# Moving the resolvents ahead in the prologue of a fused convolution, state-space and mixture-of-experts kernel

## The chip, the cores and the metric

The kernel runs on one core of a Trainium2 chip. The core's engines run their own instruction streams and meet only at semaphores: TensorE (PE in the profile), VectorE (DVE), ScalarE (ACT), GpSimd (POOL) and SyncE (SP), which issues most of the DMA transfers. The metric is the device time of one launch in microseconds; lower is better. All inputs are float32, and nearly every matrix product is made from three matmuls on high and low parts.

## The reference, cut to what matters

```python
x = x + attn(cond(x, style), Lambda, p, q, Vc, Ct, Bp, D, log_step)   # x: 64 x 64 x 1024
x = x + ffn(cond2(x, style), W_base, b_base, W_router, A, B)          # top 2 of 8 experts, LoRA rank 16

def cond(x, style):                 # 4 modulated convolutions: same, up (x2, blur), same, blur + down
    for i, typ in enumerate(TYPES):
        s = style @ mw[i].T + mb[i]
        weight = SCALE * w[i] * s[:, None, :, None]
        weight = weight * rsqrt(sum(weight ** 2) + EPS)
        x = conv(x, weight, typ) + b[i]

def s4_kernel(Lambda, p, q, B, Ct, step, L):        # inside attn, once for all rows
    Omega = exp(-2j * pi * arange(L) / L)
    g, c = 2 / step * ((1 - Omega) / (1 + Omega)), 2 / (1 + Omega)
    denom = g[:, None] - Lambda[None, :]            # 1024 roots x 64 states, complex
    cauchy = lambda v: (v[None, :] / denom).sum(-1) # four of them: k00, k01, k10, k11
    return ifft(c * (k00 - k01 / (1 + k11) * k10)).real
```

Attention is a long causal convolution of each row with this kernel K, which the program does as products with a Toeplitz matrix of K.

## The kernel before, in words

The 64 samples of the first block (`cond` and the state-space convolution) are taken in 32 tiles of two, then again 32 tiles for the second block (`cond2` and the experts). A tile g passes through a software pipeline whose steps have one function per engine with the same name: `scaled1` and `step1` and `composed1` and `step2` and `composed_out` build that tile's composed weights (taps), DMA moves them into `vm_f`, `composed2` splits them into `vm_h` and `vm_l`; `inputs` scales and splits the input into `xs_h` and `xs_l`; `layer0` makes the first convolution; `pair` and `third` the composed rest; `turn` transposes; `s4` applies the Toeplitz matrix. The main loop `body(i)` of every engine runs i from 1 to 65. What comes before it is written out by hand, one list of calls per engine named `first_turns` (GpSimd has its list ahead of and in `body(-1)`), and the order of each list is the order on that engine. That prologue also does what is needed only once:

- The style tables `tabs` (scales, and shifts by `shifts`), and a chain for the bias constants: three small TensorE products `constant(0, 0)`, `(0, 1)`, `(0, 2)` with the weights summed over their taps (`wsum`, made by GpSimd in `tap_sums` and `tap_sums_end`), each followed by `through(0, l)` on VectorE, which makes the right side of the next product.
- The edge columns, in four TensorE steps `edge_pe0` to `edge_pe3`, each followed by VectorE's `edge_ve0` to `edge_ve3`. `edge_ve0` ends in the pads, which `edge_pads_first` splits; its semaphore `apad_ready` is what ScalarE's `layer0(0)` waits for. The folds of the edge matrices `em` are GpSimd's `folded(1)` and `folded(2)`.
- The state-space kernel: `denominators` and `denominators_turned` (VectorE) make the complex denominators, ScalarE squares them, `resolvents` adds the squares and takes the reciprocal, `resolvents_scaled` makes `res`, TensorE's `resolved` sums over the states (eight products of 128x128 with 16 columns), VectorE's `transfer` (some 40 instructions of 8 columns) combines them, then TensorE and VectorE alternate in `transform`, `twiddles`, `twisted`, `transposed`, `second_transform` and `kernel_out`.

GpSimd's order for tile 1 is `inputs(1)` (writes `xs_l`), `column_sums_low(0)` (`as_l`), `pair_sums(0)` (`vm_f`), `pair_sums_low(0)` (`vs_l`). ScalarE's order after its `layer0(0)` is `composed1(1)`, `composed2(0)`, `inputs(1)`, `inputs_high(1)`, `column_sums(0)`, `pads(0)`, `pair_sums(0)`, `pair_evacuated(0, 0)`.

Of the kernel before, what the change touches and what calls it, by code (L numbers as in the profile page):

```python
# [404 lines left out]
def program(nc, d, out, sb, sem, sh):  # L405
# [57 lines left out]
    with ExitStack() as early:  # L463
        def tb(name, shape, dt=F32):
# [71 lines left out]
    mats_hi, mats_lo = sem("mats_hi"), sem("mats_lo")  # L536
    rate_ready, rate_out, den_ready, sq_ready, res_ready = (sem("rate_ready"), sem("rate_out"), sem("den_ready"),
                                                            sem("sq_ready"), sem("res_ready"))
    pe_F, at_ready, pe_dft, z_ready, pe_zT, zT_ready, pe_K, k_ready = (
        sem("pe_F"), sem("at_ready"), sem("pe_dft"), sem("z_ready"), sem("pe_zT"), sem("zT_ready"), sem("pe_K"), sem("k_ready"))  # L540
    zero_set, k_out, toep_in, pe_toep = sem("zero_set"), sem("k_out"), sem("toep_in"), sem("pe_toep")
# [71 lines left out]
    def turn_is(i, *which):  # L613
        return i in which
# [77 lines left out]
    with nc.Block() as block:  # L692
# [126 lines left out]
        def _(pool):  # L819
# [34 lines left out]
            def tap_sums(c):  # L854

                pool.wait_ge(fold_in, 32)
                for l, s in enumerate(summed(c)):
                    for h in range(2):
                        ins = G.tensor_tensor(wsum[:, l, c, h, :], s[:, 0, :], s[:, 1, :], ALU.add)
                ins.then_inc(wsum_step, 1)  # L860
# [77 lines left out]
            def body(i):  # L938
# [34 lines left out]
                if turn_is(i, 9):  # L973
                    r_low(1)
                if turn_is(i, -1):
                    pool.wait_ge(in_lo, 1)
                    tap_sums(0)
                    tap_sums_end(0)
                    folded(1, fold1())
                    folded(2, fold3())  # L980

                    inputs(1)
                    column_sums_low(0)
                    pair_sums(0)
                else:
                    if here(i + 1):
                        pair_sums(i + 1)
                        column_sums_low(i + 1)
                    if here(i + 2):
                        inputs(i + 2)  # L990
# [4 lines left out]
        def _(act):  # L995
# [170 lines left out]
            def first_turns():  # L1166
# [4 lines left out]
                inputs_high(0)  # L1171
                composed1(0)
                edge_lay_first(nc, act, sh)
                terms_of(fold1()[2:])
                act.wait_ge(den_ready, 1)
                A(tmp, den, ACT.Square).then_inc(sq_ready, 1)
                scaled1(1)
                terms_of(fold3())
                layer0(0)
# [87 lines left out]
        def _(ve):  # L1267
# [139 lines left out]

            def resolvents():
                ve.wait_ge(sq_ready, 1)
                link(V.tensor_tensor(tmp[:, 0, :], tmp[:, 0, :], tmp[:, 1, :], ALU.add))  # L1410
                link(V.reciprocal(tmp[:, 1, :], tmp[:, 0, :]))

            def resolvents_scaled():
# [215 lines left out]
            def first_turns():  # L1629
# [15 lines left out]
                edge_scale(nc, ve, sh, 0, xgA[:, 0:EB, :])  # L1645
                denominators()
                composed1(0)
                shifts(0)
                state_vectors()
                denominators_turned()  # L1650
                through(0, 0)
                composed_out(0)
                scaled1(1)
                edge_ve0(nc, ve, sh, 0, ps_p)
                edge_pads_first(nc, ve, sh)
                through(0, 1)
                resolvents()
                through(0, 2)
                state_halves()
                composed1(1)  # L1660
                resolvents_scaled()
                layer0(0)
                composed2(0)
                transfer()
                edge_ve1(nc, ve, sh, 0, ps_p)
                twiddles()
# [102 lines left out]
        def _(pe):  # L1769
# [184 lines left out]
            def first_turns():  # L1954

                step1(0)
                constant(0, 0)
                step2(0)
                edge_pe0(nc, pe, sh, 0, ps_p)
                layer0(0)  # L1960
                constant(0, 1)
                pe.wait_ge(blur, at(0))
                step1(1)
                constant(0, 2)
                pe.wait_ge(folds, 1)
                edge_pe1(nc, pe, sh, 0, ps_p)
                resolved()
                pair(0, 0)
                step2(1)
                pair(0, 1)  # L1970
# [143 lines left out]
```

## Time and profile before

| | |
|---|---|
| time, median of 3 runs | 1338.35 us (1337.68 to 1340.94) |
| the profiled execution's own time | 1339.31 us, span in the trace 1337.5 us |
| PE busy | 1295.4 us, 97% |
| DVE busy | 1044.6 us, 78% |
| ACT and POOL busy | 798.4 and 807.0 us, 60% each |
| granted TensorE clock, mean | 0.994 of full speed |

The span is cut in 40 slices of 33.4 us in the page. In the first three TensorE is busy for 3, 7 and 8 tenths, and from the fourth on for 9 tenths or more. A row of the timeline has the start and the duration in us, then engine, line, operation, written and read tile, their shapes and the count; in brackets the idle time before it and who ended it. Durations of neighbours overlap a little, since an instruction's end is counted when its writes have landed. A row of the windows view gives a stretch, the busy time of each engine, and the granted TensorE clock (1.00 is 2.4 GHz, 0.50 is 1.2 GHz).

### The profile page before, as it was taken

How to read it: one execution, taken by the hardware profiler on the slowest of the kernel's cores; microseconds unless marked ns; L12 is line 12 of the kernel's file. 1: busy time of each engine (PE TensorE's matmuls, PEld its weight loads, DVE VectorE, ACT ScalarE, POOL GpSimd, SP SyncE). 2: the span in 40 equal slices, each digit the busy share in tenths (PEclk: the TensorE clock that was granted, in tenths of full speed). 3: DMA queues.
4: the chain of work that ended last, by engine and by line, in shares of the span. 5: the costliest groups of instructions: out<-in, count | busy, mean ns of one | idle time of the engine just before them, and what ended most of it. 6: DMA issues, size and time to landing. Idle time of an engine off the chain costs nothing.

```text
span 1337.5 us, 22885 instructions
## 1 busy us (share of the span) xinstructions
PE 1295.4 (97%) x8127; PEld 1227.3 (92%) x8127; DVE 1044.6 (78%) x2442; ACT 798.4 (60%) x1625; POOL 807.0 (60%) x611
## 2 busy tenths in 40 slices
PE   3789999999999999999999999999999999999998
PEld 2689899899899999899999999999999999999998
DVE  7868878778877778778788888787878878787873
ACT  4577787778777787775545544555554454555440
POOL 6468887666676677665555545554555555545542
PEclk9889999999999999999999999999999999999999
DMA  4234444444455654452542523425243342524422
GB/s 133 74 107 132 133 133 133 133 132 133 132 146 150 151 152 134 133 154 78 125 110 91 141 77 108 124 77 153 78 127 105 100 131 78 147 85 122 110 86 87
DMA packets 86274, 158.20 MB, mean 118 GB/s; under 512 B 26633, under 2 KB 48402, under 8 KB 86034
## 3 DMA queue, kind: packets, MB, share of 16 engines
q1 hardware_dynamic: 84898, 154.79, 41.8%
q10 hardware_dynamic: 1264, 1.96, 0.5%
q8 instruction: 65, 1.06, 0.4%
q14 instruction: 47, 0.39, 0.1%
HBM read 93.79 MB, written 33.56 MB: 95 GB/s over the span
## 4 chain that ended last, share of the span: by engine, by line
PE 84%; DVE 7%; POOL 4%; ACT 3%; issue 1%; DMA 0%; SPq 0%; DVEq 0%; POOLq 0%; ACTq 0%
PE psum L1775 27%; PE psum L1777 26%; PE psum L1776 26%; PE psum L1889 2%; DVE psum L1549 2%; POOL xs_l L931 1%; ACT xin L1104 1%; DVE a_l L1525 1%; DVE a_f L1530 1%; POOL vs_l L926 0%; POOL vbuf L910 0%; POOL vbuf L906 0%; PE psum L283 0%; POOL as_l L935 0%; ACT xs_h L1109 0%
## 5 line engine op out<-in xcount | busy, mean ns | idle before, releaser
L1775 PE MATMUL psum<-wt_h,u_h 128*128 128x386 f32 (+1 forms) x760 | 261.0, 343 | 0.0
L1777 PE MATMUL psum<-wt_h,u_l 128*128 128x386 f32 (+1 forms) x760 | 258.1, 340 | 0.0
L1776 PE MATMUL psum<-wt_l,u_h 128*128 128x386 f32 (+1 forms) x760 | 257.8, 339 | 0.0
L1549 DVE STREAM_TRANSPOSE psum<-vbuf 32x256 f32<-32x256 f32 x480 | 218.9, 456 | 11.8 <-ACT vbuf L1141 0.7
L1525 DVE SCALAR_TENSOR_TENSOR a_l<-psum,tabs,a_h 128x512 fp32r<-128x512 f32 x128 | 95.9, 751 | 160.2 <-ACT a_h L1123 160.1
L906 POOL TENSOR_TENSOR vbuf<-vbuf 128x512 f32<-128x512 f32 x64 | 97.1, 1517 | 191.4 <-ACT vbuf L1155 191.4
L920 POOL TENSOR_TENSOR vm_f<-vm_f 128x512 f32<-128x512 f32 x64 | 82.8, 1293 | 180.4 <-DVE vm_l L1519 180.1
L1148 ACT ACTIVATE vbuf<-psum,tabs 128x512 f32<-128x512 f32 x128 | 105.2, 822 | 118.0 <-PE psum L1777 114.0
L1775 PE MATMUL psum<-a_h,vm_h 128*128 128x256 f32 x512 | 148.7, 290 | 3.2 <-ACT vbuf L1148 3.0
L1776 PE MATMUL psum<-a_l,vm_h 128*128 128x256 f32 x512 | 146.3, 286 | 0.0
L1777 PE MATMUL psum<-a_h,vm_l 128*128 128x256 f32 x512 | 146.0, 285 | 0.0
L1775 PEld LDWEIGHTS psum<-wt_h,u_h 128*128 128x128 f32 x760 | 143.9, 189 | 2.1
L931 POOL TENSOR_TENSOR xs_l<-xin,xs_h 128x1024 fp32r<-128x1024 f32 x64 | 142.4, 2225 | 4.8 <-ACT xs_h L1109 4.8
L1776 PEld LDWEIGHTS psum<-wt_l,u_h 128*128 128x128 f32 x760 | 143.6, 189 | 1.2
L1777 PEld LDWEIGHTS psum<-wt_h,u_l 128*128 128x128 f32 x760 | 143.3, 189 | 0.0
L949 POOL TENSOR_TENSOR xo<-xr,xo 128x1024 f32<-128x1024 f32 x32 | 85.4, 2667 | 93.3 <-DMA xo<-in_b_base_dram 93.3
L1537 DVE TENSOR_TENSOR u_l<-psum,u_h 128x1024 fp32r<-128x1024 f32 x64 | 78.3, 1223 | 41.8 <-ACT u_h L1163 41.7
L1775 PE MATMUL psum<-xs_h,m_h 128*128 128x512 f32 x256 | 104.0, 406 | 0.0
L1775 PEld LDWEIGHTS psum<-a_h,vm_h 128*128 128x128 f32 x512 | 98.5, 192 | 4.4 <-ACT vbuf L1148 3.7
L1776 PE MATMUL psum<-xs_l,m_h 128*128 128x512 f32 x256 | 101.1, 395 | 0.0
L1777 PE MATMUL psum<-xs_h,m_l 128*128 128x512 f32 x256 | 101.0, 394 | 0.0
L910 POOL TENSOR_TENSOR vbuf<-vbuf 128x512 f32<-128x512 f32 x64 | 97.9, 1530 | 5.0
(309 smaller groups left out, 3806.8 us busy)
## 6 DMA issues: line engine op xcount, KB each, us to landing
vm_f<-vv SPq DMA_DIRECT2D x256, 112.0 KB, 4.4
xin<-in_x_ph_dram SPq DMA_DIRECT2D x32, 512.0 KB, 5.0
xr<-in_x_row_dram SPq DMA_DIRECT2D x32, 512.0 KB, 4.1
x1d<-xr SPq DMA_DIRECT2D x64, 256.0 KB, 3.3
xin<-x1d SPq DMA_DIRECT2D x32, 512.0 KB, 5.3
xr<-x1d SPq DMA_DIRECT2D x64, 256.0 KB, 5.9
xo<-in_b_base_dram SPq DMA_DIRECT2D x32, 512.0 KB, 5.8
out_dram<-xo SPq DMA_DIRECT2D x31, 512.0 KB, 2.9
```

The source lines that it names most:

```text
L906: G.tensor_tensor(v3[:, :, 1:H:2], v3[:, :, 1:H:2], by_odd, ALU.subtract).then_inc(v3_odd, 1)
L910: G.tensor_tensor(v3[:, :, 0:H:2], v3[:, :, 0:H:2], by_odd, ALU.add).then_inc(v3_val, 1)
L920: G.tensor_tensor(vs_f, vm_f[:, :, :, 0, :], vm_f[:, :, :, 1, :], ALU.add).then_inc(vs_sum, 1)
L931: G.tensor_tensor(xs_l[:, :, 1:H + 1], xin[:, :, :], xs_h[:, :, 1:H + 1].bitcast(F32), ALU.subtract).then_inc(in_lo, 1)
L949: G.tensor_tensor(xo[:, :].rearrange("p (n q) -> p n q", q=2), xr[:, :, :].rearrange("p q n -> p n q"), xo[:, :].rearrange("p (n q) -> p n ...
L1148: A(view(vbuf, H * b, (2 * H + b - H * b, 2), (2, Q)), ps_pair.rearrange("p (r m) -> p r m", r=2), ACT.Identity, scale=tab(c, t, b, T_S4), ...
L1525: V.scalar_tensor_tensor(out=by_parity(a_l, b), in0=ps_x[:, b, :].rearrange("p (m r) -> p r m", r=2), scalar=tabs[:, c, T_S1, batch(t, b)] ...
L1537: V.tensor_tensor(u_l[:, :, :, :].rearrange("m k b c -> m b k c"), ps_x[:, :, :].rearrange("m b (k c) -> m b k c", c=C), u_h[:, :, :, :].r ...
L1549: ins = V.transpose(ps_x[to, :, :].rearrange("p b (k n) -> p b k n", n=P)[:, :, :, frm], v3[frm, :, :].rearrange("p b (k n) -> p b k n", n ...
L1775: nc.tensor.matmul(to, stat_h, mov_h, start=first_ and n == 0, stop=False, skip_group_check=True)
L1776: nc.tensor.matmul(to, stat_h, mov_l, start=False, stop=False, skip_group_check=True)
L1777: ins = nc.tensor.matmul(to, stat_l, mov_h, start=False, stop=end, skip_group_check=True)
```

## The change

All of it lies in the prologue. On VectorE the chain from the denominators to `res` is put in one piece behind `composed1(0)`, with `state_vectors`, `state_halves` and `composed_out(0)` in it; `shifts(0)`, `through(0, 0)`, `scaled1(1)`, the edge step and `layer0(0)` follow, and `through(0, 1)` and `(0, 2)` stand behind `layer0(0)`. On ScalarE the square moves ahead of four small terms. On TensorE `resolved` moves ahead of `constant(0, 0)`, which both stand behind `layer0(0)` now. GpSimd waits with its tap sums until the first resolvent instruction is done (`res_begun`), and with its folds until `res` is.

```diff
 # GpSimd, body(-1)
                 if turn_is(i, -1):
+
                     pool.wait_ge(in_lo, 1)
+                    pool.wait_ge(res_begun, 1)
                     tap_sums(0)
                     tap_sums_end(0)
+                    pool.wait_ge(res_ready, 1)
                     folded(1, fold1())
                     folded(2, fold3())
 # ScalarE
                 edge_lay_first(nc, act, sh)
-                terms_of(fold1()[2:])
                 act.wait_ge(den_ready, 1)
                 A(tmp, den, ACT.Square).then_inc(sq_ready, 1)
+                terms_of(fold1()[2:])
                 scaled1(1)
 # VectorE
             def resolvents():
                 ve.wait_ge(sq_ready, 1)
-                link(V.tensor_tensor(tmp[:, 0, :], tmp[:, 0, :], tmp[:, 1, :], ALU.add))
+                V.tensor_tensor(tmp[:, 0, :], tmp[:, 0, :], tmp[:, 1, :], ALU.add).then_inc(res_begun, 1)
+                ve.wait_ge(res_begun, 1)
                 link(V.reciprocal(tmp[:, 1, :], tmp[:, 0, :]))
...
                 denominators()
                 composed1(0)
+                denominators_turned()
+                state_vectors()
+                state_halves()
+                composed_out(0)
+                resolvents()
+                resolvents_scaled()
                 shifts(0)
-                state_vectors()
-                denominators_turned()
                 through(0, 0)
-                composed_out(0)
                 scaled1(1)
                 edge_ve0(nc, ve, sh, 0, ps_p)
                 edge_pads_first(nc, ve, sh)
+                layer0(0)
                 through(0, 1)
-                resolvents()
+                composed1(1)
+                composed2(0)
                 through(0, 2)
-                state_halves()
-                composed1(1)
-                resolvents_scaled()
-                layer0(0)
-                composed2(0)
                 transfer()
 # TensorE
                 step1(0)
-                constant(0, 0)
                 step2(0)
                 edge_pe0(nc, pe, sh, 0, ps_p)
                 layer0(0)
-                constant(0, 1)
+                resolved()
+                constant(0, 0)
                 pe.wait_ge(blur, at(0))
                 step1(1)
+                constant(0, 1)
                 constant(0, 2)
                 pe.wait_ge(folds, 1)
                 edge_pe1(nc, pe, sh, 0, ps_p)
-                resolved()
                 pair(0, 0)
```

VectorE before, around the resolvents (`apad` are the pads that end the edge step, `xmid` the small right side of the constants, `dt` the squares and their reciprocal, `res` what TensorE waits for in `resolved`, `a_l` is `layer0`):

```order
L350 TENSOR_TENSOR apad_l<-apadf,apad_h 128x128
L1328 TENSOR_TENSOR xmid<-psum,tabs 128x64
L1331 TENSOR_TENSOR xmid<-xmid,tabs 128x64
L1410 TENSOR_TENSOR dt<-dt 128x512
L1411 RECIPROCAL dt<-dt 128x512
```

VectorE with the change, at the same instructions (all line numbers are 4 or 5 higher; the first `xmid` row waits for `constant(0, 0)`, the pads follow nine rows further on):

```order
L1414 TENSOR_TENSOR dt<-dt 128x512
L1416 RECIPROCAL dt<-dt 128x512
L1419 TENSOR_TENSOR res<-dt 128x512
L1420 SCALAR_TENSOR_TENSOR res<-dt 128x512
L1422 MEMSET roots 128x1
L1320 TENSOR_TENSOR tabs<-sty,vec 128x64
L1321 MEMSET tabs 128x128
L1322 TENSOR_TENSOR tabs<-sty,vec 128x64
L1323 TENSOR_SCALAR tabs<-tabs 64x64
L1324 TENSOR_SCALAR tabs<-tabs 64x64
L1325 TENSOR_SCALAR tabs<-tabs 128x64
L1332 TENSOR_TENSOR xmid<-psum,tabs 128x64
```

The pads stood ahead of the reciprocal, and stand behind it, behind `res` and behind the first `xmid` now.

TensorE before, from the end of `step1(1)` to the first product of `pair(0, 0)` (`vbd<-res` is `resolved`, `xmid,wsum` a constant, `ae,em` is `edge_pe1`):

```order
L1776 MATMUL psum<-y_l,cm_h 128x256
L1777 MATMUL psum<-y_h,cm_l 128x256
L1797 MATMUL psum<-xmid,wsum 128x64
L276 MATMUL psum<-ae,em 128x256 x2
L1804 MATMUL psum<-vbd,res 128x16 x8
L1775 MATMUL psum<-a_h,vm_h 128x256
```

TensorE with the change, from the end of `layer0(0)` to the first products of `step1(1)`:

```order
L1781 MATMUL psum<-xs_l,m_h 128x512
L1782 MATMUL psum<-xs_h,m_l 128x512
L1809 MATMUL psum<-vbd,res 128x16 x8
L1802 MATMUL psum<-tabs,wsum 128x64
L1780 MATMUL psum<-y_h,cm_h 128x256
L1781 MATMUL psum<-y_l,cm_h 128x256
```

`resolved` has gone from just ahead of `pair(0, 0)` to ahead of the first constant, which used to be TensorE's first product after `step1(0)`.

## Rows read from the trace of the kernel before

**Rows 1.** Part 2 of the page: PE's busy tenths in 40 slices
```profile
PE   3789999999999999999999999999999999999998
```

**Rows 2.** Timeline of PE: start us, duration, operation, [idle before <-releaser]
```profile
27.55 0.69 PE L1797 MATMUL psum<-tabs,wsum 64*128 64x64 f32 x2 [6.69 <-POOL wsum L866]
...
34.95 0.39 PE L1777 MATMUL psum<-xs_h,m_l 128*128 128x512 f32 x1
...
43.13 3.59 PE L1804 MATMUL psum<-vbd,res 128*128 128x16 f32 x16 [5.12 <-DVE res L1415]
46.57 0.56 PE L1775 MATMUL psum<-a_h,vm_h 128*128 128x256 f32 x1
...
57.41 1.58 PE L283 MATMUL psum<-de,em 128*64 128x384 f32 x4
```

**Rows 3.** Timeline of DVE
```profile
22.56 1.41 DVE L1316 TENSOR_TENSOR tabs<-sty,vec 128x64 f32<-128x64 f32 x1
...
24.99 0.22 DVE L1347 COPY yv<-ssm 128x2 f32<-128x2 f32 x1
...
27.63 0.82 DVE L1403 SCALAR_TENSOR_TENSOR dt<-roots,ssm,dt 128x512 f32<-128x512 f32 x1
...
30.97 0.62 DVE L1514 COPY vv<-psum 128x448 f32<-128x448 f32 x1 [1.25 <-PE psum L1777]
31.51 0.60 DVE L1495 SCALAR_TENSOR_TENSOR y_l<-x1w,tabs,y_h 128x128 fp32r<-128x128 f32 x2
32.57 0.50 DVE L325 TENSOR_TENSOR psum<-psum,tabs 128x320 f32<-128x320 f32 x1 [0.46 <-PE psum L268]
...
34.70 0.55 DVE L350 TENSOR_TENSOR apad_l<-apadf,apad_h 128x128 fp32r<-128x128 f32 x1
35.73 0.23 DVE L1328 TENSOR_TENSOR xmid<-psum,tabs 128x64 f32<-128x64 f32 x1 [0.49 <-PE psum L1797]
...
36.86 3.35 DVE L1411 RECIPROCAL dt<-dt 128x512 f32<-128x512 f32 x1
...
41.80 0.68 DVE L1414 TENSOR_TENSOR res<-dt 128x512 f32<-128x512 f32 x1
...
46.77 0.23 DVE L1429 COPY fs<-psum 128x64 f32<-128x64 f32 x1 [0.37 <-PE psum L1804]
...
47.46 1.24 DVE L1422 TENSOR_TENSOR cx<-fs 128x8 f32<-128x8 f32 x1
...
49.53 1.20 DVE L1424 TENSOR_TENSOR cx<-cx 128x8 f32<-128x8 f32 x1
...
53.96 0.17 DVE L1451 TENSOR_SCALAR atv<-cx 128x8 f32<-128x8 f32 x1
```

**Rows 4.** Timeline of ACT
```profile
35.34 0.29 ACT L1120 ACTIVATE a_f<-apad_h,apad_l 128x1 f32<-128x1 f32 x1 [1.35 <-PE psum L1777]
...
40.60 1.06 ACT L1109 ACTIVATE xs_h<-xin 128x1024 fp32r<-128x1024 f32 x1
...
48.72 0.63 ACT L1098 ACTIVATE vs_h<-vm_f 128x512 fp32r<-128x512 f32 x1 [2.66 <-POOL vm_f L920]
```

**Rows 5.** Timeline of POOL
```profile
21.25 2.63 POOL L931 TENSOR_TENSOR xs_l<-xin,xs_h 128x1024 fp32r<-128x1024 f32 x1 [0.68 <-ACT xs_h L1109]
...
47.40 1.29 POOL L920 TENSOR_TENSOR vm_f<-vm_f 128x512 f32<-128x512 f32 x1
49.42 1.28 POOL L926 TENSOR_TENSOR vs_l<-vm_f,vs_h 128x512 fp32r<-128x512 f32 x1 [0.74 <-ACT vs_h L1098]
...
68.50 1.19 POOL L935 TENSOR_TENSOR as_l<-a_f,as_h 128x512 fp32r<-128x512 f32 x1
69.64 2.20 POOL L931 TENSOR_TENSOR xs_l<-xin,xs_h 128x1024 fp32r<-128x1024 f32 x1
```

**Rows 6.** Windows of 1 us: stretch and length, busy of each engine, PEclk, DMA
```profile
42.00:43.00 1.00, 0.00 (x0) 0.00 (x0) 1.00 (x2) 0.00 (x0) 1.00 (x1) 0.55 0.03 8
...
72.00:73.00 1.00, 0.19 (x2) 0.00 (x0) 0.96 (x3) 0.97 (x4) 1.00 (x1) 0.91 0.36 41
```

More of the change, by code:

```diff
@@ L538, in program @@
                                                             sem("sq_ready"), sem("res_ready"))
+    res_begun = sem("res_begun")
     pe_F, at_ready, pe_dft, z_ready, pe_zT, zT_ready, pe_K, k_ready = (
```

## The prediction

> **What bounds the kernel now.** I read the page's busy tenths first. TensorE is full from the fourth slice on and only the first three are not [rows 1]; the change touches nothing behind them. So the question is by how many microseconds the start of the full stretch shifts; TensorE has no room later to give or take them. Then I read TensorE's timeline of the head for its waits. The reader is to see three: 6.69 us for GpSimd's tap sums ahead of the first constant, 5.12 us for `res` ahead of `resolved`, and then that `pair(0, 0)` starts as soon as `resolved` is done, at 46.57 [rows 2]. Next VectorE's timeline [rows 3]: `transfer` runs from 46.77 to 54.13, and it feeds the edge step whose product starts on TensorE at 57.41 [rows 2]. From there to the full stretch it is one chain, and I take its length as unchanged. So the measure is the end of `transfer`: 54.13 now.
>
> **What the change removes.** TensorE no longer waits for the tap sums. `step2(0)` can follow `c1_l` at about 22.7 instead of 28.2, and `layer0(0)`, 7.1 us after that (28.24 to 35.34, [rows 2]), ends at about 30. `resolved` leaves the place ahead of `pair(0, 0)`. But ScalarE's `layer0(0)` began at 35.34, not when the product was done but when the pads were (VectorE's `apad_l`, 34.70 + 0.55 = 35.25) [rows 3, 4]. An earlier product brings nothing unless the pads come earlier.
>
> **When the pads come.** This is the sum, on VectorE:
> - `denominators_turned` comes up at 22.56 and is held like the instruction that stood there, to 23.9, since GpSimd's `xs_l` runs to 23.88 [rows 3, 5]. The pair takes 1.3 like the pair of `res` (41.80 until TensorE starts at 43.13) [rows 2, 3]: 25.2. ScalarE's square hides under what follows.
> - `state_vectors` 24.99 to 27.63, so 2.6; with `state_halves` 0.2, less some 0.4 for a GpSimd that is silent now: 27.6. The copy of the taps, 0.6, its product long done: 28.2.
> - The sum of squares 0.7, by the like `res` product: 28.9. Reciprocal 3.35: 32.3. `res` 1.3: 33.6, against 43.1 before [rows 3]. GpSimd's tap sums run beside the reciprocal and are done by 33, for nothing.
> - TensorE runs `resolved`: 46.57 - 43.13 = 3.44 at the 0.50 clock of that stretch [rows 2, 6]; about 1.7 at the full one (half, an estimate). Which? It will have been idle for 3.6 us. It lost the clock after 4 us of idleness (last product at 38.0, 0.55 in the window from 42) and, in the window from 72, after much shorter gaps [rows 6]. I take the half clock: 37.1. Ends: 35.3 and 37.1.
> - Then `constant(0, 0)`, 0.5 (the wait ahead of `xmid`), `through(0, 0)` 0.5 (two of 0.23), `y_l` 0.6, and `edge_ve0` with the pads 35.25 - 32.57 = 2.7 [rows 3]: 41.4. GpSimd's folds, behind `res` now, hold some of these small instructions; none to 0.9, I take 0.3. `shifts(0)` runs under `resolved`, cover enough: six small instructions in 3.4 us; at 1.7 us it just fills.
>
> So the pads come at 41.7, 6.4 late (40.0 at the full clock, 4.7 late).
>
> **What hangs on them.** ScalarE is a strict list: `layer0(0)`, taps, `inputs(1)`, `xs_h`, which ended 41.66 - 35.34 = 6.3 after its start [rows 4]. Now 48.1. GpSimd follows with `xs_l` 2.2, `as_l` 1.2 and the pair sums 1.3 [rows 5]: 52.9 (with 0.1 for a wait). ScalarE's `vs_h` 0.6, GpSimd's `vs_l` 1.3: about 54.9, against 50.70 before. Before, `xs_l` ran ahead of `transfer`, under `res` and `a_l`.
>
> Now `transfer`. VectorE gets there after `layer0(0)`, two constants' steps and `vm_l`, at about 48: `pe_F` no longer makes it wait. But the four GpSimd instructions lie right over it. The trace shows what that does: an 8-column `cx` product, 0.16 us by itself, took 1.24 us and ended at 48.70, when GpSimd's pair sum ended at 48.69; another took 1.20 and ended at 50.73, with `vs_l` at 50.70 [rows 3, 5]. `transfer` takes 7.36, of which such holds are 2.4 (0.3, 1.1, 1.0), so 4.95 by itself. With holds through `xs_l`, `as_l` and the pair sum it makes little way before 52.9, does some 0.9 of its work until `vs_l`, and the rest, 3.9, from 54.9 on: end at 58.7, 4.6 later than 54.13.
>
> The Trainium skill (SBUF — State Buffer, Who interferes with whom) says it as a rule: a VectorE instruction with two SBUF inputs and a GpSimd instruction that reads SBUF exclude each other, and whichever comes second is blocked for the whole of the first. By that rule all four instructions hold `transfer` and the end is 58.7; by the two long holds that the trace shows, and no more, it would be 53.2 or, where TensorE is the later one, 54.8. No row here shows four in a row.
>
> TensorE meanwhile: `pair(0, 0)` waits for ScalarE's `pads(0)`, about 49.2; with 5.1 us for it and `step2(1)` (46.57 to 51.67), and a wait of `pair(0, 1)` for the evacuation behind `vs_h` (54.3), it is done with `pair(0, 1)` near 56.5, before `transfer`. So `transfer` decides, by 2 us.
>
> Nothing else is priced: no instruction is added but semaphore waits; SP's tap transfer goes out 3 us earlier, the next `xin` load 4 to 6 us later than now but still 15 us before it is wanted.
>
> **The sum.** Against the profiled execution (span 1337.5, own time 1339.31, 0.96 above the median 1338.35) it is +4.6; on the median 1338.35 + 4.6 = 1343.0.
>
> **Rivals.**
> - A, the forecast: half clock in `resolved`, GpSimd holds `transfer`: +4.6, 1343.0. Chance 0.35, its own range 1341.5 to 1344.
> - B, TensorE keeps the full clock through the idle 3.6 us: every step from the pads on is 1.7 less less 0.3 for `shifts`: +3.2, 1341.6. For it: the window holds products on both sides of the gap. Against: rows 6. Chance 0.25.
> - C, not slower, the other side: VectorE slips between GpSimd's instructions, so that `transfer` is held as little as before. At the full clock the pads come at 40.0, `xs_h` at 46.4, the pair sum at 51.2, `vs_h` 51.8, evacuation 52.6, `pair(0, 1)` to 54.6, and TensorE's list decides: +0.7, 1339.1. It decides as soon as `transfer` is held under 3 us in all. For it: GpSimd's `xs_l` at 41.80 took 3.3 us where one at 69.64 took 2.2 [rows 5], so VectorE can win too. Chance 0.15.
> - D, a second loss of the clock. TensorE has 2 to 3 us of idleness ahead of `transform` that it has not now. If the clock falls there, the edge product and the 12 products of 512 columns of `layer0(1)` run at half speed (512 columns are 0.21 us at 2.4 GHz), at most 2.6 + 1; I take 2.5 to 3 on top of A: +7.5, 1345.9. Chance 0.20.
> - E, faster: the loss of the clock in the window from 72 [rows 6] does not come again with the shifted head. It costs 2 to 3 us there, so with C it gives -2, and past -4 only with a head that is shorter by 2 besides. Chance 0.05.
>
> **The numbers.** A measurement of this kernel tells a change from none at about 0.3%, 4.0 us, so the bounds are 1334.3 and 1342.4. Slower holds most of A (0.28 of 0.35), a fifth of B (0.05), D (0.20) and 0.02 of errors that all share: 0.55. Faster 0.05. Within: 0.40. The range runs from C to D with a little of each bound: 1338.8 to 1346.5.
>
> **What would show it.** Right: `step2(0)` at 22.7; `res` at 33.6; `apad_l` at 40 to 42, with TensorE between `resolved` and `step1(1)` waiting for VectorE; `xs_h` at 46 to 48; several `cx` instructions of `transfer` over 1 us long that end with a GpSimd instruction; `transfer` ending at 57 to 59 and the `de,em` product at 60.5 to 62. Wrong: pads before 39 (then `through(0, 0)` didn't wait for `resolved`), or `transfer` shorter than 7 us with GpSimd running beside it (then C), or a tail of the head that takes up the shift, with the same start of the full stretch.

## The result and the profile after

The changed kernel takes 1341.16 us (median of 20 runs, 1339.55 to 1343.69); the kernel before, run beside it, 1339.25 us (20 runs, 1336.92 to 1341.31). The ratio is 1.0016, with a 95% interval from 1.0009 to 1.0023: slower by 1.2 to 3.1 us, which is inside the 0.3% that the prediction took as the bound of no change. Forecast were +4.6 us (1343.0) in a range from 1338.8 to 1346.5. So the sign and the range held, and the size was too large by a factor of about two (4.6 for 1.9 between the medians).

The profiled execution's own time is 1340.23 us, its span 1338.4 us. The page, with its busy time, its tenths in 40 slices and the granted clock:

```profile
PE 1295.9 (97%) x8127; PEld 1227.8 (92%) x8127; DVE 1044.4 (78%) x2442; ACT 797.7 (60%) x1625; POOL 804.3 (60%) x611
...
PE   4789999999999999999999999999999999999998
...
PEclk9699999999999999999999999999999999999999
```

TensorE's tenths differ from [rows 1] in the first slice alone: 4 for 3, since work has moved into it. The second slice has as much as before and, with a clock digit of 6, a good part of it at half speed. TensorE's busy time is the same to 0.5 us. So the head has to answer.

TensorE's timeline of the head, to be laid beside [rows 2]:

```profile
22.64 0.60 PE L1780 MATMUL psum<-r_h,c_h 128*128 128x320 f32 x1 [1.93 <-DVE c_l L1508]
...
32.86 2.94 PE L1809 MATMUL psum<-vbd,res 128*128 128x16 f32 x16 [2.85 <-DVE res L1420]
35.73 0.69 PE L1802 MATMUL psum<-tabs,wsum 64*128 64x64 f32 x2
38.18 0.55 PE L1780 MATMUL psum<-y_h,cm_h 128*128 128x256 f32 x1 [1.77 <-DVE y_l L1500]
...
44.86 0.66 PE L1802 MATMUL psum<-xmid,wsum 64*128 64x64 f32 x2 [4.44 <-DVE xmid L1335]
...
52.92 0.39 PE L1780 MATMUL psum<-a_h,vm_h 128*128 128x256 f32 x1 [1.01 <-ACT vbuf L1152]
...
56.99 0.40 PE L1815 MATMUL psum<-atv,roles 128*128 128x16 f32 x2 [2.35 <-DVE atv L1456]
...
61.03 1.59 PE L283 MATMUL psum<-de,em 128*64 128x384 f32 x4
```

The wait for the tap sums is gone: `step2(0)` starts at 22.64. `resolved` starts at 32.86 instead of 43.13. Most of the ten microseconds comes back as waits for VectorE: 1.77, 4.44 and 2.35 us, the last of them for `transfer`. The edge product starts at 61.03 instead of 57.41.

VectorE's timeline, beside [rows 3]:

```profile
28.07 3.35 DVE L1416 RECIPROCAL dt<-dt 128x512 f32<-128x512 f32 x1
32.13 0.68 DVE L1420 SCALAR_TENSOR_TENSOR res<-dt 128x512 f32<-128x512 f32 x1
36.52 0.23 DVE L1332 TENSOR_TENSOR xmid<-psum,tabs 128x64 f32<-128x64 f32 x1 [2.07 <-PE psum L1802]
40.02 0.29 DVE L350 TENSOR_TENSOR apad_l<-apadf,apad_h 128x128 fp32r<-128x128 f32 x1
46.99 2.11 DVE L1339 TENSOR_SCALAR tabs<-xmid 128x64 f32<-128x64 f32 x1
49.13 0.21 DVE L1434 COPY fs<-psum 128x64 f32<-128x64 f32 x1
49.38 0.91 DVE L1425 TENSOR_TENSOR cx<-fs 128x8 f32<-128x8 f32 x1
50.28 1.25 DVE L1427 TENSOR_TENSOR cx<-fs 128x8 f32<-128x8 f32 x1
52.35 1.19 DVE L1429 TENSOR_TENSOR cx<-cx 128x8 f32<-128x8 f32 x1
56.77 0.16 DVE L1456 TENSOR_SCALAR atv<-cx 128x8 f32<-128x8 f32 x1
```

The pads end at 40.31 (35.25 before), behind a wait of 2.07 us for the constant that stands behind `resolved`. `transfer` runs from 49.13 to 56.93. ScalarE, beside [rows 4]:

```profile
40.41 0.30 ACT L1124 ACTIVATE a_f<-apad_h,apad_l 128x1 f32<-128x1 f32 x1 [9.34 <-DVE apad_l L350]
...
45.67 1.06 ACT L1113 ACTIVATE xs_h<-xin 128x1024 fp32r<-128x1024 f32 x1
...
51.54 0.63 ACT L1102 ACTIVATE vs_h<-vm_f 128x512 fp32r<-128x512 f32 x1 [4.09 <-POOL vm_f L921]
```

and GpSimd, beside [rows 5]:

```profile
46.87 2.19 POOL L932 TENSOR_TENSOR xs_l<-xin,xs_h 128x1024 fp32r<-128x1024 f32 x1 [7.94 <-ACT xs_h L1113]
49.02 1.24 POOL L936 TENSOR_TENSOR as_l<-a_f,as_h 128x512 fp32r<-128x512 f32 x1
50.21 1.29 POOL L921 TENSOR_TENSOR vm_f<-vm_f 128x512 f32<-128x512 f32 x1
52.25 1.28 POOL L927 TENSOR_TENSOR vs_l<-vm_f,vs_h 128x512 fp32r<-128x512 f32 x1 [0.74 <-ACT vs_h L1102]
```

Read the ends of the two lists together. VectorE's long small instructions end at 49.10, 50.29, 51.53 and 53.54; GpSimd's four end at 49.06, 50.26, 51.50 and 53.53. Each is a VectorE instruction of 0.16 to 0.20 us that waited out one of GpSimd. The first is no part of `transfer`: it is the last instruction but one of the third constant, a tensor_scalar with one input. That it too is held agrees with the Trainium skill (SBUF — State Buffer, Who interferes with whom), by which a tensor_scalar can take the shared ports in a fast mode.

What becomes of the shift later is read at one instruction that every tile has, VectorE's `a_f` of `layer0`. Its start, less that in the profile before, in us:

| tile | 1 | 2 | 35 | 50 | 63 |
|---|---|---|---|---|---|
| changed | 3.62 | 2.73 | 2.88 | 1.60 | 0.79 |
| before, profiled again | 1.70 | 1.07 | 1.64 | 0.13 | -0.63 |
| changed, profiled again | 4.73 | 4.42 | 4.84 | 3.53 | 2.77 |

From tile 2 to tile 35 the shift stands still to 0.6 us, as argued. Two executions of one kernel differ by 1 to 2 us in the head and by as much again later; so a pair of profiles gives the mechanism, and only the medians give the size. Of the two pairs the first has +2.73 at tile 2, the second 4.42 - 1.07 = +3.35.

### The profile page after: what moved, and what is told of

Read it like the earlier page. It is cut to its first block, busy times and chain, and to the rows that moved or that the text cites. A ratio compares the mean times of both kernels' runs of the same rounds, so it can differ in the third digit from the quotient of the medians.

```text
span 1338.4 us, 22886 instructions
## 1 busy us (share of the span) xinstructions
PE 1295.9 (97%) x8127; PEld 1227.8 (92%) x8127; DVE 1044.4 (78%) x2442; ACT 797.7 (60%) x1625; POOL 804.3 (60%) x611
## 3 DMA queue, kind: packets, MB, share of 16 engines
q10 hardware_dynamic: 1264, 1.96, 0.5%
## 4 chain that ended last, share of the span: by engine, by line
PE 87%; DVE 7%; ACT 2%; POOL 2%; issue 1%; DMA 1%; SPq 0%; ACTq 0%; DVEq 0%; POOLq 0%
PE psum L1780 28%; PE psum L1782 27%; PE psum L1781 27%; PE psum L1894 2%; DVE psum L1554 1%; DVE vm_l L1524 1%; POOL xs_l L932 0%; DVE a_l L1530 0%; DVE a_f L1535 0%; PE psum L283 0%; DMA vm_f<-vv 0%; ACT xin L1108 0%; ACT a_h L1127 0%; DVE c_l L1508 0%; POOL vs_l L927 0%
```

## The experiments

My theory: the pads come late because `through(0, 0)` waits for a constant behind `resolved`; ScalarE's list carries this to GpSimd, whose four instructions then hold `transfer`. This is theory P of the expectations. Rivals: that TensorE's own list with its lost clock sets the end of the head (theory T, and D of the prediction), that the waits put on GpSimd cost the time, and that it is the place of the resolvents on VectorE alone. All ratios are to the kernel before, run beside each experiment, with 95% intervals; the changed kernel's own was 1.0016. Differences between two experiments come from different ratios and are less certain than the ratios.

**The pads ahead of the resolvents** (e1), VectorE's list of the changed kernel:

```diff
                 composed_out(0)
+                edge_ve0(nc, ve, sh, 0, ps_p)
+                edge_pads_first(nc, ve, sh)
                 resolvents()
...
                 scaled1(1)
-                edge_ve0(nc, ve, sh, 0, ps_p)
-                edge_pads_first(nc, ve, sh)
                 layer0(0)
```

> The changed kernel with edge_ve0 and the pads moved back ahead of the resolvents on VectorE. Theory P (the pads are late behind the resolvents and resolved, so ScalarE's list and GpSimd's four instructions come late and hold transfer): pads at about 31, layer0 on ScalarE from 31, xs_h at 37, res at 36 instead of 32.8, GpSimd's folds till 41.6 and xs_l after them; transfer from 46 to 53 instead of 49 to 57; the time falls by about 3 to 4 us against the changed kernel, to 0 to 1 below the kernel before. Theory T (TensorE's own list with its lost clock sets the end of the head, not the pads): res is 3 later, nothing is won, 0 to +3 against the changed kernel.

Measured: 1341.37 us, 1.0020 [1.0010, 1.0030]. No gain. From the timelines of VectorE and ScalarE:

```profile
29.95 0.29 DVE L350 TENSOR_TENSOR apad_l<-apadf,apad_h 128x128 fp32r<-128x128 f32 x1
...
43.24 0.73 ACT L1086 ACTIVATE c_h<-psum,tabs 128x192 fp32r<-128x192 f32 x2 [9.35 <-PE psum L1782]
46.26 1.06 ACT L1113 ACTIVATE xs_h<-xin 128x1024 fp32r<-128x1024 f32 x1
```

The pads were there at 30.24, ten microseconds sooner, and `xs_h` came 0.6 us later than in the changed kernel. ScalarE stood for 9.35 us at its next piece, `composed1(1)`, which needs `step1(1)`; and that needs `y_l`, which VectorE still made behind `through(0, 0)`, at 40.37. So the theory was half of it: two things that ScalarE's list needs stood behind `resolved`, and taking away one uncovers the other. By its time alone this run came out as theory T had it; the rows tell the two apart.

**The constant ahead of `resolved`** (e2), TensorE's list:

```diff
                 layer0(0)
-                resolved()
                 constant(0, 0)
+                resolved()
```

> The changed kernel with constant(0, 0) ahead of resolved on TensorE, so that through(0, 0) no longer waits for resolved. Theory P: the constant runs at 31.7, beside the reciprocal; pads at 37.6 instead of 40.3, xs_h 44, transfer ends 54.3 instead of 56.9, time 2.7 us below the changed kernel, level with the one before. Theory T: no difference within 0.5 us, since resolved, which starts no earlier, is all that TensorE has there.

Measured: 1340.68 us, 1.0010 [1.0001, 1.0019]. Both the pads and `y_l` are freed from `resolved` here: the pads end at 38.62 (1.7 us sooner), `xs_h` at 45.03 (1.7 sooner), `transfer` at 55.4 (1.5 sooner), the edge product starts at 59.55 (1.5 sooner). The time fell by 0.5 us between the medians (0.8 by the ratios), less than the interval resolves, where 2.7 was expected. The chain as far as `transfer` is as the theory says; the whole of it doesn't arrive, and the table behind e9 shows where it stays. The constant started only at 32.09, after 1.87 us for the tap sums, which the change puts beside the reciprocal.

**Without the two waits of GpSimd** (e3):

```diff
-                    pool.wait_ge(res_begun, 1)
                     tap_sums(0)
                     tap_sums_end(0)
-                    pool.wait_ge(res_ready, 1)
                     folded(1, fold1())
```

> The changed kernel without GpSimd's two waits (tap sums and folds follow xs_l at once, from 24 to 31). Theory P: state_vectors 0.4 slower, the resolvents' two-input instructions held by at most 0.5 each, the pads 0.5 to 1 less held behind them; sum 0 +- 0.5 us. Rival, that the waits carry the change: every two-input instruction of the resolvents is held by a fold, res 1.5 to 3 later and the time 1.5 to 3 us above the changed kernel.

Measured: 1345.42 us (5 runs), 1.0048 [1.0034, 1.0062]: 4 us slower than the changed kernel, and the two intervals don't touch. The waits pay for themselves. VectorE, GpSimd and TensorE:

```profile
28.03 3.21 POOL L897 TENSOR_TENSOR em<-em,xr 64x128 f32<-64x128 f32 x6
...
29.51 3.35 DVE L1414 RECIPROCAL dt<-dt 128x512 f32<-128x512 f32 x1
31.32 3.69 POOL L897 TENSOR_TENSOR em<-em,xo 64x128 f32<-64x128 f32 x6
...
34.75 3.60 PE L1807 MATMUL psum<-vbd,res 128*128 128x16 f32 x16 [5.03 <-DVE res L1418]
```

The reciprocal starts 1.44 us later (the small state vectors are held, several at 0.35 us), the two `res` products take 0.93 and 0.94 us instead of 0.75 and 0.68, and `resolved`, after 5.03 us of idleness, runs wholly at half speed. The pads end at 42.36 and `transfer` at 59.1, 2.2 later than in the changed kernel; tile 2 starts 5.1 later. I had priced the waits at nothing, as ordering that costs or brings no more than 0.5 us.

**`xs_l` behind `transfer`** (e4), GpSimd's list:

```diff
-                    inputs(1)
-                    column_sums_low(0)
                     pair_sums(0)
+                    column_sums_low(0)
+                    pair_sums_low(0)
+                    pool.wait_ge(at_ready, 1)
+                    inputs(1)
```

(`body(0)` leaves out its own `pair_sums_low(0)`; that line is not shown.)

> The changed kernel with GpSimd's order pair sums, as_l, vs_l, and xs_l(1) behind the end of transfer (a wait for at_ready). Pads and xs_h don't move. Theory P with holds through the shared port: the 2.1 us hold under xs_l goes, transfer ends at 55 instead of 56.9, the time is 1.5 to 2 us below the changed kernel. Theory T, or holds that only fill idle time of VectorE: the end of transfer and the time stay within 0.5 us.

Measured: 1341.73 us, 1.0017 [1.0008, 1.0027]. VectorE, GpSimd and TensorE from the third constant on:

```profile
45.62 1.32 DVE L1339 TENSOR_TENSOR xmid<-xmid,vec 128x64 f32<-128x64 f32 x1
46.98 1.08 DVE L1341 TENSOR_SCALAR tabs<-xmid 128x64 f32<-128x64 f32 x1
47.98 1.31 DVE L1342 TENSOR_SCALAR tabs<-xmid 128x64 f32<-128x64 f32 x1
49.21 0.21 DVE L1436 COPY fs<-psum 128x64 f32<-128x64 f32 x1
...
54.01 0.16 DVE L1458 TENSOR_SCALAR atv<-cx 128x8 f32<-128x8 f32 x1
54.26 2.18 POOL L932 TENSOR_TENSOR xs_l<-xin,xs_h 128x1024 fp32r<-128x1024 f32 x1 [5.02 <-DVE atv L1458]
...
55.35 1.10 DVE L1427 TENSOR_TENSOR cx<-cx,roles 128x8 f32<-128x8 f32 x1
...
59.27 2.82 PE L283 MATMUL psum<-de,em 128*64 128x384 f32 x4
```

With no GpSimd instruction beside it `transfer` takes 4.96 us instead of 7.80: the 2.8 us of holds are shown, and so is the 4.95 that the prediction worked out for `transfer` by itself. But the three instructions that went ahead now hold the last three of the third constant, by 1.09, 0.88 and 1.13 us, so `transfer` starts no sooner (49.21 for 49.13). It ends 2.8 us sooner, and only 1.7 of that is the order: the other 1.1 was there before, at the third constant's first row (45.62 for 46.73), since `resolved` ran at the full clock in this execution (1.96 us). The time doesn't move. The deferred `xs_l` holds the twiddles (1.10 us for 0.16), and the clock was at half from 55.9 to 62.8, so that the edge product starts 1.8 sooner but takes 2.82 us instead of 1.59.

**Pads, `y_l` and `step1(1)` all ahead, and GpSimd's four instructions ahead of the second folds** (e5), cut to its core:

```diff
 # VectorE
                 composed_out(0)
+                scaled1(1)
+                edge_ve0(nc, ve, sh, 0, ps_p)
+                edge_pads_first(nc, ve, sh)
                 resolvents()
                 resolvents_scaled()
+                layer0(0)
                 shifts(0)
                 through(0, 0)
-                scaled1(1)
-                edge_ve0(nc, ve, sh, 0, ps_p)
-                edge_pads_first(nc, ve, sh)
-                layer0(0)
-                through(0, 1)
                 composed1(1)
+                through(0, 1)
                 composed2(0)
 # TensorE
                 layer0(0)
-                resolved()
-                constant(0, 0)
                 pe.wait_ge(blur, at(0))
                 step1(1)
+                constant(0, 0)
+                resolved()
 # GpSimd
                     folded(1, fold1())
-                    folded(2, fold3())
                     inputs(1)
-                    column_sums_low(0)
                     pair_sums(0)
+                    column_sums_low(0)
+                    pair_sums_low(0)
+                    pool.wait_ge(vs_lo, 1)
+                    pool.wait_ge(z_ready, 1)
+                    folded(2, fold3())
```

> The changed kernel with all that ScalarE waits for ahead of the resolvents: VectorE does y_l of tile 1, edge_ve0 and the pads first, and layer0(0) right behind res; TensorE does step1(1) and constant(0, 0) ahead of resolved; GpSimd does xs_l, the pair sums, as_l and vs_l ahead of the second folds, which wait for the end of twiddles. Theory P: ScalarE's layer0 from 31.5, xs_h 38, GpSimd's four instructions from 38 to 45, transfer from 43 to 49 or 50, held by one or two of them only; TensorE's list then sets transform at 51, so 3 us below the kernel before (1336) and 5 below the changed kernel. Rival C, that the clock and TensorE's list set the head whatever VectorE does: within 1 us of the changed kernel.

Measured: 1337.42 us, 0.9993 [0.9982, 1.0003]. The pads end at 31.77, `xs_h` at 38.2, `xs_l` at 42.4; `transfer` runs from 48.05 to 53.9 and the edge product starts at 57.15, with the clock at full speed there. `transfer` starts 5 us later than expected: the first constant waited 5.24 us for the tap sums and started at 36.04, `xs_l` held one of the `tabs` instructions for 2.05 us, and `vs_l` still lies over the first product of `transfer` (1.00 us). This is the first experiment whose median isn't above the kernel before, and its ratio is 0.23% under the changed kernel's. Run once more:

> e5_pads_and_step once more, on whatever chip this call gets: 1.5 to 2.5 us below the kernel before if its first result holds, and its interval then leaves out 1; within 0.5 us of it if the first was chance.

1337.69 us, 0.9988 [0.9979, 0.9997]. The first interval holds 1, the second leaves it out.

**The same without GpSimd's part** (e6): the VectorE and TensorE edits above, GpSimd's list as in the changed kernel.

> The same orders on VectorE and TensorE, GpSimd's order as in the changed kernel (both folds ahead of xs_l). Theory P: folds until 42.4, the four instructions from there to 49, beside transfer again: transfer from 43.5 to 52, time 1 to 2 us below the kernel before. If the late xs_h alone mattered and not what lies beside transfer, it is as fast as the run with the other GpSimd order.

Measured: 1340.18 us, 1.0007 [0.9998, 1.0016]. `transfer` from 48.14 to 54.1, nearly as in e5, but the clock was lost from 53.6 to 60.4 and the edge product starts 1.4 later, at 58.56, and takes 2.41 us. So GpSimd's order is worth 2.7 us here between the medians (1.9 by the ratios), and the orders of VectorE and TensorE about 1. These two intervals (e5 and e6) overlap between 0.9998 and 1.0003, so the split is less certain than its direction. And the gain isn't `transfer` itself, whose end differs by 0.2 us: it is the stretch at half speed behind it, which e5 doesn't have. Why GpSimd's order should decide that isn't shown; TensorE waited 2.82 us for `transfer` in e6 and 1.22 in e5, since `pair(0, 1)` was done sooner in e6.

**The clock kept up** (e7), TensorE's list of the changed kernel, with 30 products into a PSUM tile whose result nobody reads:

```diff
                 pair(0, 1)
+                for _ in range(5):
+                    product(ps_third[:, 0:Q], [(vm_h[:, 1, P * r:P * r + P], vm_l[:, 1, P * r:P * r + P],
+                                                a_h[:, 1, 1:1 + Q], a_l[:, 1, 1:1 + Q]) for r in range(2)], True, True)
                 transform()
```

> The changed kernel with 30 more matmuls of 256 columns between pair(0, 1) and transform, whose products nobody reads, in the 2.4 us that TensorE idles there (they take 3 to 3.5 us at the full clock). Where the lost clock from 57 to 61 counts: the clock stays at 1.00, third(0, 0) to second_transform run at full speed, the edge product starts at 60 to 60.5 instead of 61.0 and the time falls by 0.5 to 1 us, less up to 1 us that the filler itself may stand in the way. Where only VectorE's transfer counts: the edge product's start moves by less than 0.3 and the time not at all.

Measured: 1341.16 us, 1.0015 [1.0006, 1.0024]: no change. Windows (stretch and length, busy time of the engines, then the granted clock, DMA share and GB/s) of the changed kernel and of this experiment:

```profile
60.00:64.00 4.00, 4.00 (x15) 2.12 (x15) 2.27 (x6) 1.66 (x3) 2.06 (x2) 0.88 0.14 32
76.00:80.00 4.00, 2.15 (x10) 2.15 (x11) 3.97 (x8) 3.25 (x6) 1.96 (x2) 0.75 0.37 131
53.00:90.00 37.00, 30.01 (x157) 24.32 (x158) 25.68 (x80) 24.39 (x52) 16.39 (x13) 0.91 0.23 68
```

```profile
60.00:64.00 4.00, 4.00 (x17) 2.31 (x17) 2.27 (x6) 1.58 (x4) 2.59 (x3) 1.00 0.30 66
76.00:80.00 4.00, 2.92 (x13) 2.92 (x14) 4.00 (x7) 2.48 (x4) 1.27 (x1) 0.50 0.30 116
53.00:90.00 37.00, 32.05 (x183) 26.83 (x182) 25.11 (x78) 23.97 (x50) 15.87 (x12) 0.91 0.24 68
```

The filler kept the clock at 1.00 past the edge product. But it didn't make the time at half speed less, it moved it. A mean of 0.75 over 4 us is 2.0 us at 1.2 GHz; counted so, the windows from 72 to 84 have 3.4 us at half speed in the changed kernel and 6.8 with the filler, and from 53 to 90 both have the same mean, 0.91. The kernel before has 0.91 there too.

Nor did the filler bring the edge product forward. It starts at 60.25, 0.78 sooner, but `transfer` had ended 0.68 sooner in this execution, at 56.25, and the filler stood in the way:

```profile
56.08 0.17 DVE L1456 TENSOR_SCALAR atv<-cx 128x8 f32<-128x8 f32 x1
57.39 0.29 PE L1815 MATMUL psum<-atv,roles 128*128 128x16 f32 x2
```

Its products ran 1.1 us past the end of `transfer`. At tile 2 the two kernels stand at +2.72 and +2.73. So this run is no test of what a loss of the clock costs; it shows that this filler, at this place, brings nothing. The table in *TensorE: Matmul & The Clock Gate*, Why this matters for your kernels (the Trainium skill), advises against idle gaps between bursts; the clock was indeed kept by filling one, and was down for longer afterwards.

**Constant first and GpSimd's order** (e8): e2 and the GpSimd part of e5 together.

> The changed kernel with constant(0, 0) ahead of resolved and GpSimd's four instructions ahead of the second folds, which wait for twiddles. Theory P: xs_h at 44.2 as with the constant alone, so the four instructions still lie beside transfer; the folds were done long before, so nothing but a small gain: transfer ends at 55 to 55.4, time within 0.7 us of the run with the constant alone. If GpSimd's order alone is worth the difference, 2 us or more below it.

Measured: 1340.15 us, 1.0009 [1.0000, 1.0018]. `transfer` from 48.27 to 55.1, the edge product at 59.29. It is 0.5 us under e2, which the intervals don't tell apart. GpSimd's order brings little while `xs_h` comes at 45: its four instructions still fall on the third constant (2.11 and 1.32 us for 0.20 and 0.18) and on `transfer`. It pays once `xs_h` is early (e5).

**`step2(1)` early as well** (e9): e5, and on top of it

```diff
 # VectorE
                 resolvents_scaled()
-                layer0(0)
                 shifts(0)
-                through(0, 0)
+                layer0(0)
                 composed1(1)
-                through(0, 1)
+                through(0, 0)
                 composed2(0)
+                through(0, 1)
                 through(0, 2)
 # TensorE
                 resolved()
+                step2(1)
                 constant(0, 1)
...
                 pair(0, 0)
-                step2(1)
                 pair(0, 1)
```

> As e5_pads_and_step, with step2(1) behind resolved on TensorE, where it idled 2.3 us, and with shifts(0) ahead of layer0(0) and c_l and vm_l between the constants on VectorE. Theory P: vm_l at 43 instead of 44.2, so GpSimd's pair sum, as_l and vs_l end at 47.7 instead of 49.3, transfer ends at 52 instead of 53.9 and pair(0, 1) is done by then; time 1 to 2 us below e5_pads_and_step. If the constants' round trips set the start of transfer, no gain: within 0.5 us.

Measured: 1336.72 us, 0.9982 [0.9974, 0.9991], which is clear of both kernels: 2.4 us under before (1.2 to 3.5), and some 4.5 under the changed one. Against e5, run again beside it, it is 1.0 us less, and those intervals overlap. VectorE, ScalarE and GpSimd:

```profile
30.88 0.29 DVE L350 TENSOR_TENSOR apad_l<-apadf,apad_h 128x128 fp32r<-128x128 f32 x1
...
36.53 1.06 ACT L1116 ACTIVATE xs_h<-xin 128x1024 fp32r<-128x1024 f32 x1
...
45.56 1.26 POOL L927 TENSOR_TENSOR vs_l<-vm_f,vs_h 128x512 fp32r<-128x512 f32 x1
47.25 0.22 DVE L1437 COPY fs<-psum 128x64 f32<-128x64 f32 x1
...
52.06 0.16 DVE L1459 TENSOR_SCALAR atv<-cx 128x8 f32<-128x8 f32 x1
```

GpSimd's last instruction ends at 46.82 and `transfer` starts at 47.25: nothing lies over it, and it takes 4.97 us, as in e4. It ends at 52.22, 4.7 us sooner than in the changed kernel, and the edge product starts at 56.26.

**Both kernels profiled once more**, since one profile each had carried the comparison:

> The kernel before once more, for its profile. Where the clock of the head falls and rises at other moments from one execution to the next: the first u_l tiles and the end of the head move by up to 1 us against the first profile, and so do the small gaps of the second block (turns 36 to 38 and 55), which are then no part of the change. Otherwise every start up to 100 us agrees within 0.3 us.

> The changed kernel once more, for its profile. pads at 39 to 40.5, transfer 7.5 to 8 us long with at least three cx or tabs instructions over 0.9 us, the clock lost between 56 and 61; tile 2 of layer0 2 to 3.5 us later than in the profiles of the kernel before.

Measured: 1338.84 and 1342.07 us, one execution each. The changed kernel repeats its head (pads at 40.1, `transfer` 48.93 to 56.8 with holds of the same sizes, edge product 61.26). The kernel before was expected to agree with its first profile to 0.3 us, and doesn't: it is 1.7 us later. First, the row of GpSimd in the first profile of before, which began in the same hundredth as VectorE's 0.68 us `res` product [rows 3]:

```profile
41.80 3.31 POOL L931 TENSOR_TENSOR xs_l<-xin,xs_h 128x1024 fp32r<-128x1024 f32 x1 [4.15 <-ACT xs_h L1109]
```

and both in the second profile:

```profile
41.47 2.17 POOL L931 TENSOR_TENSOR xs_l<-xin,xs_h 128x1024 fp32r<-128x1024 f32 x1 [4.15 <-ACT xs_h L1109]
41.98 2.20 DVE L1414 TENSOR_TENSOR res<-dt 128x512 f32<-128x512 f32 x1
```

In the first VectorE passed and GpSimd was stretched by 1.1 us; in the second GpSimd began half a microsecond sooner, and VectorE's product, 1.5 us late, ended half a microsecond behind it. `resolved` went from 43.13 to 44.84, the end of `transfer` from 54.13 to 55.82, the edge product from 57.41 to 59.11. It is the same program: who comes first decides, as the Trainium skill has it (SBUF — State Buffer, Who interferes with whom: issue order decides who is blocked). The first profile of before, on which the prediction rests, was one with the lucky head. That luck doesn't reach the end: the second execution, with the later head, was 0.5 us shorter in all (1338.84 against 1339.31).

All fourteen profiles on one table. The second column is the end of `transfer`, the next two are the time from there to the start of the edge product and to `a_f` of tile 2, in us, and the last is the mean granted clock from 53 to 90 us:

| | `transfer` ends | to the edge product | to tile 2 | clock |
|---|---|---|---|---|
| before | 54.13 | 3.28 | 30.39 | 0.91 |
| before, again | 55.82 | 3.29 | 29.77 | 0.91 |
| changed | 56.93 | 4.10 | 30.32 | 0.91 |
| changed, again | 56.76 | 4.50 | 32.18 | 0.82 |
| e1 | 56.79 | 3.95 | 31.50 | 0.86 |
| e2 | 55.43 | 4.12 | 31.40 | 0.86 |
| e3 | 59.15 | 4.15 | 33.17 | 0.81 |
| e4 | 54.17 | 5.10 | 33.86 | 0.82 |
| e5 | 53.85 | 3.30 | 29.52 | 0.95 |
| e5, again | 53.53 | 3.28 | 29.51 | 0.95 |
| e6 | 54.07 | 4.49 | 32.11 | 0.82 |
| e7 | 56.25 | 4.00 | 30.99 | 0.91 |
| e8 | 55.14 | 4.15 | 30.36 | 0.91 |
| e9 | 52.22 | 4.04 | 30.28 | 0.95 |

Two things set tile 2, and with it the time: when `transfer` ends, and how long the chain behind it is. That chain runs from 29.5 to 33.9 us, and it is long where the clock was down for long. So e2's gain is 1.5 us sooner at `transfer` less a chain longer by 1.1, and e4's is 2.8 less 3.5 (0.9 of it the held twiddles). And e9 against the changed kernel is the nearest to a clean pair: the chains behind `transfer` are equally long to 0.04 us, `transfer` ends 4.7 us sooner, and the medians lie 4.4 apart.

## Why the prediction was right, and where its size was off

- **`step2(0)` at 22.7, `res` at 33.6.** Measured 22.64 and 32.86 (33.77 in the second profile). Right. 0.7 of what the forecast was too late comes from here in the first.
- **`resolved` at half clock, 3.44 us.** The mis-sized term of the sum. It took 2.94 in the first profile, where the granted clock fell in its course, and 1.96 in the second, where it stayed up nearly to its end. The idleness ahead of it, 2.85 us, was less than the 3.6 that the prediction took. Between forecast A (half clock) and rival B (full clock) the two profiles lie on either side, and on their ends, about 35.8 in both, nearer to B (35.3) than to A (37.1).
- **Pads at 41.7.** Measured 40.31 and 40.1, within the 40 to 42 named; the wait of VectorE for the constant behind `resolved` was there (2.07 us). But that the pads are *the* thing ScalarE waits for was only half right: e1 shows that `y_l` is a second one, at the same place.
- **The hold of `transfer` by four instructions.** Right, and shown by e4. The holds are 0.75 + 1.08 + 1.03 = 2.86 us inside `transfer`, and 1.9 on the third constant's instruction ahead of it. Its rest after `vs_l` took 3.4 us where 3.9 was forecast: 1.6 us of its own work was done by then and not 0.9, some of it in the gap ahead of `vs_l` and some between the holds. Rival C, that VectorE slips through and TensorE's list decides, is out: TensorE waited 2.35 us for `transfer`. (The 53.2 that the prediction gives for two long holds doesn't follow from its terms: 48 + 4.95 + 2.1 is 55.1.) `transfer` ended at 56.93 instead of 58.7: +2.8. Of the 1.8 missing, 1.4 was there at the pads and 0.4 is this.
- **The chain behind `transfer` as unchanged.** Right in the first pair of profiles (30.39 and 30.32 us to tile 2) and wrong in the second (29.77 and 32.18). The second loss of the clock (D) did come, in both profiles of the changed kernel. In the first it was short: the edge product starts 3.62 later for a `transfer` that ends 2.80 later, and the next stretch at half speed is shorter in return, 3.4 us instead of 6.8, so that tile 2 is at +2.73. In the second it was longer, nothing was returned (0.54 from 80 to 84 us, where the first has 0.82), and with `transfer` ending at the same time tile 2 and the execution's own time are 1.7 and 1.8 us later. So D's mechanism was true, and its price was between nothing and 2 us, from one execution to the next, where the prediction had 2.5 to 3.
- **GpSimd's waits at nothing.** Wrong by 4 us (e3), though not in the sum: the kernel that ran has them. Of the 5.1 us by which e3 is later at tile 2, 2.2 are there at `transfer` and 2.9 come behind it. The waits are a part of the change that works.
- **The reference.** The forecast took one profile of before as the kernel. Against it the changed kernel is +2.73 at tile 2; against the second profile of before, +1.66 in the first profile of the changed kernel and +3.35 in the second. The measured +2 lies between. How often before has the lucky head wasn't measured. It matters for the cause: in the first pair the whole shift at tile 2 is there at `transfer` (2.80), in the second 0.94 is, and 2.41 come from the chain behind. Both causes are in the traces; their shares in the median are open.
- **What was luck.** The range held, and the mechanism as far as `transfer` is the one that was forecast. But 1341.16 lies below A's own range (1341.5 to 1344), the time came out within the 0.3% that had 0.40 and not above it, which had 0.55, and the sum holds a `transfer` that is too late by 1.8 us and no loss of the clock behind it. These two errors work against each other.

Where the intended gain went: `res` is 10 us earlier, and everything that uses it but `resolved` itself stands in lists behind other things. VectorE's next work (pads, `y_l`) was put behind TensorE's product of `res`; through ScalarE's list this delays GpSimd, whose work then falls on `transfer`. The gain became a wait, and the wait a contention. e9 puts what ScalarE needs ahead of the resolvents, and leaves `transfer` alone.

Open: why executions of one kernel part by 1 to 2 us again in the second block (the shift to the first profile fell between tiles 35 and 50 in every profile taken later, by 1.0 to 1.8 us, so that step, too, may be the first profile's own); what decides whether the clock is lost behind `transfer`, and for how long; and what a kernel with `transfer` as late as the changed one and no loss of the clock would take: e7 had that, but with the filler in the way.

## What to carry to other kernels

When a piece is moved ahead in strictly ordered lists, ask of every engine what its next instruction waits for, and then again of the one behind it; freeing one of two waits at the same place brings nothing. A chain of small instructions with two inputs in SBUF is a bad neighbour of GpSimd: here each GpSimd instruction of 1.24 to 2.19 us cost it 0.75 to 1.9 us. e9 had all of GpSimd's work ahead of the chain, and that paid; where a part was moved only a little ahead (e4), it held the instructions before the chain instead. And before pricing a few microseconds from one profile, take two, and split the shift at the step that you argue about: a race for the ports in the head moved this one by 1.7 us, and the chain behind `transfer` differed by 1.9 us between two executions of one program.

## What the runs showed of the hardware

- An 8-column product of 0.16 us took 1.25 us beside a GpSimd instruction of 1.29 us, and in e1 2.15 us beside one of 2.19; a tensor_scalar of 64 columns with a single SBUF input took 2.11 us beside one of 2.19. Between two GpSimd instructions in a row none, one or two small ones of VectorE went through.
- Sixteen passes of 16 columns are busy time in the trace (windows of 1.00), yet the granted clock fell during them (2.94 us, after 2.85 idle), and in another execution of the same program only at their end (1.96 us, after 2.22 idle).
- A loss of the clock in a head that waits for VectorE's chain put the edge product 0.8 us later in one execution and 1.2 in another, against the kernel before (4.10 and 4.50 us behind `transfer` for 3.28), and tile 2 by nothing in the one and by about 2 us in the other.
- A filler of 30 products kept the granted clock at 1.00 where it had fallen to half, and it was down for longer afterwards: 0.91 from 53 to 90 us with and without it.
